# Four-layer model on one core: product-key expert products in one-pass parts, streamed tables, joined stage fronts

## The chip, the core and the metric

The kernel runs on one core of one Trainium2 chip. TensorE (PE) multiplies matrices, VectorE (DVE), ScalarE (ACT) and GpSimd (POOL) work on elements, SyncE's queue (SP) issues the transfers between DRAM and the on-chip memory (SBUF). Each engine runs its own program; semaphores order them. The metric is the device time of one execution in microseconds (us), less is better.

## The reference, cut to what matters

`x` is 64 sequences of 64 tokens with 256 channels (4096 tokens, float32). Four layers follow; each adds an attention and a feed-forward part to `x`, each on a layer norm of `x`:

```python
x = x + _L0_xattn_ref(_layernorm(x), ctx, mask, ...)   # attention with 8-bit rounded values
x = x + _L0_ffn_ref(_layernorm(x), Wq, keys, e_down, e_up)   # product-key experts
x = x + _L1_xattn_ref(...); x = x + _L1_ffn_ref(...)   # linear attention; 4-bit weights + LoRA
x = x + _L2_xattn_ref(...); x = x + _L2_ffn_ref(...)   # memory attention; self-attention + 16 experts
x = x + _L3_xattn_ref(...); x = x + _L3_ffn_ref(...)   # attention; 16 experts, two of them per token
```

The product-key part, which the change touches most:

```python
q1, q2 = (q[..., 0, :], q[..., 1, :])              # 4 heads, 64 wide each
s1, i1 = jax.lax.top_k(q1 . keys[:, :, 0], 8);  s2, i2 = jax.lax.top_k(q2 . keys[:, :, 1], 8)
all_scores = s1[..., :, None] + s2[..., None, :]   # 64 candidates
final_scores, pk_idx = jax.lax.top_k(all_scores, 8)
hidden = silu(x . e_down[final_indices]) * relu(final_scores)
out = hidden . e_up[final_indices]                 # 2048 experts, tables 2048 x 256
```

The dense part of layer 1 uses `w = (q - 7.5) * scale` for its two weights, plus a LoRA product of rank 16 for each, with 1024 hidden channels.

## The kernel before

The program is a row of stages, each a block of its own; between blocks all engines meet and the stage's semaphores are cleared. In order of time: first attention (0 to 370 us, 16 units of 256 tokens, `head_attention_stage` with `quant=True`), product-key experts (370 to 1201, `peer_stage`), linear attention, dense feed-forward (from 1424, `ffn_stage` named ffn4), memory attention, self-attention (from 1786), the 16 experts of layer 2 computed for every token in two passes (moe2a, moe2b), the last attention and the routed experts (4242 to 4604). `x` stays in SBUF throughout.

**Product-key stage** (L1030 to L1451). 4096 tokens in 16 tiles of 256. It gathers no rows: for every token it computes the sums of scores for all 2048 experts (16 first keys times 128 second ones), sets those under the eighth best to zero ("mask"), transposes that table on PE and multiplies it into the dense hidden values of all 2048 experts. A tile has 8 slots of 256 experts, and each engine's order is written out by hand (`tile_pe`, `tile_act`, `tile_dve`, `tile_gp`, L1331 to L1406); three tiles are in work at once. Per slot p:

- PE: the up product (`up_pe`, L1286: 8 float32 instructions of 256 columns), 16 transposes of a part of the table (`table_pe`, L1263), in some slots norm transposes, queries or scores, and the down product of slot p-2 (`down_pe`, L1313: 8 float32 instructions of 256 columns).
- ACT: SiLU (L1295), copy of the table part (L1271), in slots 0, 1, 4, 5 the sums of heads 0 and 2 (`sums_act`, L1191, 16 small activations each), score copies (L1175).
- DVE: activations times table (`weigh_dve`, L1304) of slot p-1, in slot 0 and 3 the search for the best (`pick_dve`, with the comparison L1219), in slots 1, 2, 5, 6 two masks each (`mask_dve`, L1246), in slot 2 the copy of the normalized input (`hand_over_dve`) and the norm of the tile after next (`norm_dve`), in slot 4 the residual.
- POOL: the sums of heads 1 and 3 (`sums_pool`, L1198) in slots 0, 1, 4, 5, and a power for the norm in slot 2 (`norm_pool`, L1114).

The two expert tables `wg` (for e_down) and `wd` (for e_up) are loaded once, as float32, and stay in SBUF.

**Split products.** The dense and layer-2 stages already run a float32 product as three one-pass products: each operand is split into a rounded part hi (type fp32r) and the rest lo = value - hi, and hi\*hi, hi\*lo and lo\*hi are summed (L576, L589). For the hidden values ACT rounds (L647) and POOL subtracts (L656).

**First attention.** POOL clears the block-diagonal value buffers `vbd` before its units (L2806 to L2813), and DVE waits for that. SP loads one context tile per unit. ACT's list of a unit and POOL's mask and bias work have slack that differs from unit to unit.

**Dense stage.** `dequant_block` (L138 to L196) is a block of its own: ten loads, then on DVE scaling of both tables (L179, L180), 12 additions of LoRA products (L186), on ACT two roundings (L194, L195), on DVE two subtractions (L189). After it the stage's own block starts with the norm of the first tile.

**Self-attention.** The raw weights come through four buffers `raw`, filled by SP at the start of the block, rounded by ACT (L1613) and subtracted by DVE (L1620).

**Routed stage.** PE computes the router's logits tile by tile (8 tiles, L3540) into one PSUM bank; after the last one DVE runs a chain of 20 steps over all of them (`route_dve`, L3554 to L3581) with one exponential on ACT (L3585) near its start; the counts on PE (L3601) wait for the chain's last cast (L3577).

## Time and profile before

| | |
|---|---|
| median of 3 runs | 4598.83 us |
| the runs | 4588.35, 4598.83, 4601.52 us |
| the profiled execution | 4605.66 us |
| its span | 4603.9 us, mean granted clock of TensorE 0.936 |
| PE busy | 4047.8 us (88%) |
| PE's weight loads | 3353.4 us (73%) |
| DVE busy | 2595.6 us (56%) |
| ACT busy | 2070.3 us (45%) |
| POOL busy | 903.5 us (20%) |

The shares are means over stages with different limits, so a stage has to be read by itself. A row of a windows view gives, for a stretch of the span, its length, then for each engine the busy time and in brackets the number of instructions, then the granted clock of TensorE (1.00 is 2.4 GHz, 0.50 is 1.2 GHz), the busy share of the DMA engines and GB/s. A row of a timeline gives start and length in us, the engine, the line of the kernel, the operation, what it writes and reads, the shapes and how many instructions were joined to the row; in square brackets the idle time of that engine ahead of it and what ended it. Lengths of PE rows include the time in which an instruction overlaps the next.

### The profile page before, as it was taken

What the parts mean: (1) busy time and instruction counts of PE and PEld (TensorE: products, weight loads), DVE (VectorE), ACT (ScalarE), POOL (GpSimd) and SP (SyncE); (2) the same over time, 40 slices, a digit from 0 to 9 for tenths busy, and PEclk for the clock granted to TensorE, in tenths of its full rate; (3) what the DMA queues carried; (4) which work ended last, traced back from release to release, by engine and by line L of the source; (5) the groups of instructions that cost most, each with busy time, mean ns of one, the idle gap of its engine ahead of it and who ended that gap; (6) DMA issues with size and microseconds to landing.
All of it is one profiled execution on the core that took longest, in us unless ns stands there. A gap on an engine that the chain in (4) does not pass through costs nothing. (4 is left out here: it accounts for less than half of the span.)

```text
span 4603.9 us, 74464 instructions
## 1 busy us (share of the span) xinstructions
PE 4047.8 (88%) x25328; PEld 3353.4 (73%) x25328; DVE 2595.6 (56%) x5873; ACT 2070.3 (45%) x5341; POOL 903.5 (20%) x738
## 2 busy tenths in 40 slices
PE   6885999999896877999999997999979998887791
PEld 4554899999774765877877886788868886665671
DVE  6887989899474337444444443433333333776533
ACT  6884666666222433433433333433333333675140
POOL 1112333233000430000000000222222222001245
PEclk8997999999997997999999998999989998998595
DMA  2001000000001003000000001100010000001244
GB/s 67 14 15 44 1 0 0 0 0 1 28 21 42 0 30 115 6 6 6 6 6 6 6 5 34 34 10 9 5 54 10 9 10 24 12 12 42 84 135 127
DMA packets 100309, 119.50 MB, mean 26 GB/s; under 512 B 13792, under 2 KB 81216, under 8 KB 99776
## 3 DMA queue, kind: packets, MB, share of 16 engines
q1 hardware_dynamic: 93168, 97.25, 6.6%
q0 software_dynamic: 6864, 18.75, 1.5%
q8 instruction: 150, 2.46, 0.2%
q14 instruction: 127, 1.04, 0.1%
HBM read 93.03 MB, written 22.94 MB: 25 GB/s over the span
## 5 line engine op out<-in xcount | busy, mean ns | idle before, releaser
L1191 ACT ACTIVATE peer_tab<-peer_sims 128x128 f32<-128x128 f32 x1024 | 305.7, 393 | 0.0
L1198 POOL TENSOR_TENSOR peer_tab<-peer_sims 128x2048 f32<-128x2048 f32 x64 | 246.3, 3868 | 289.3 <-ACT peer_sims L1175 260.1
L1246 DVE SCALAR_TENSOR_TENSOR peer_tab<-peer_tab,peer_th 128x2048 f32<-128x2048 f32 x128 | 298.2, 2371 | 2.6 <-ACT peer_tab L1191 2.3
L1263 PE MATMUL bank<-ident,peer_tab 128*128 128x128 f32 x2048 | 247.9, 275 | 24.6 <-DVE peer_tab L1246 24.6
L1263 PEld LDWEIGHTS bank<-ident,peer_tab 128*128 128x128 f32 x2048 | 234.5, 142 | 37.9 <-DVE peer_tab L1246 25.4
L1673 DVE COPY mha_ks<-bank 128x512 f32<-128x512 f32 x128 | 88.4, 691 | 302.5 <-PE bank L1638 300.1
L1778 PE MATMUL bank<-mha_wo,mha_oT 128*128 128x256 f32 x1024 | 243.6, 381 | 0.0
L1313 PE MATMUL bank<-peer_wd,peer_hh 128*128 128x256 f32 x1024 | 242.0, 379 | 1.2 <-DVE peer_hh L1304 1.2
L1286 PE MATMUL bank<-peer_hT,peer_wg 128*128 128x256 f32 x1024 | 242.7, 380 | 0.0
L668 DVE TENSOR_TENSOR moe2a_b<-moe2a_a,bank 128x512 f32<-128x512 f32 x104 | 71.4, 687 | 270.9 <-PE bank L576 239.8
L1286 PEld LDWEIGHTS bank<-peer_hT,peer_wg 128*128 128x128 f32 x1024 | 195.2, 191 | 26.6
L656 POOL TENSOR_TENSOR moe2a_hh_lo<-moe2a_hh,moe2a_hh_hi 128x512 fp32r<-128x512 f32 x104 | 141.1, 1357 | 370.0 <-ACT moe2a_hh_hi L647 352.9
L668 DVE TENSOR_TENSOR moe2b_b<-moe2b_a,bank 128x512 f32<-128x512 f32 x96 | 65.9, 687 | 250.5 <-PE bank L576 219.4
L1313 PEld LDWEIGHTS bank<-peer_wd,peer_hh 128*128 128x128 f32 x1024 | 188.2, 190 | 24.1 <-DVE peer_hh L1304 1.9
L1778 PEld LDWEIGHTS bank<-mha_wo,mha_oT 128*128 128x128 f32 x1024 | 186.0, 192 | 20.2
L656 POOL TENSOR_TENSOR moe2b_hh_lo<-moe2b_hh,moe2b_hh_hi 128x512 fp32r<-128x512 f32 x96 | 130.8, 1363 | 344.5 <-ACT moe2b_hh_hi L647 333.6
L1666 ACT ACTIVATE mha_vs<-bank 128x512 f32<-128x512 f32 x128 | 76.4, 597 | 253.4 <-PE bank L1652 253.2
L1295 ACT ACTIVATE peer_a<-bank 128x512 f32<-128x512 f32 x128 | 76.2, 595 | 210.9 <-PE bank L1286 169.6
L647 ACT ACTIVATE moe2a_hh_hi<-moe2a_hh 128x512 fp32r<-128x512 f32 x104 | 65.7, 632 | 226.8 <-DVE moe2a_hh L673 209.3
L1824 POOL TENSOR_TENSOR mha_r<-mha_ms,neghalf 128x4 f32<-128x4 f32 x8 | 8.1, 1008 | 811.8 <-DVE mha_ms L1813 811.8
L1661 ACT ACTIVATE mha_qs<-bank 128x512 f32<-128x512 f32 x128 | 76.6, 599 | 196.0 <-PE bank L1638 196.0
L1304 DVE TENSOR_TENSOR peer_hh<-peer_a,peer_cwT 128x512 f32<-128x512 f32 x128 | 121.9, 953 | 75.7 <-PE bank L1313 75.7
(533 smaller groups left out, 11101.1 us busy)
## 6 DMA issues: line engine op xcount, KB each, us to landing
m_y_rows<-moe_y SPq DMA_DIRECT2D x79, 128.0 KB, 1.7
att_ctxT<-in_ctxT_dram SPq DMA_DIRECT2D x32, 256.0 KB, 2.7
lin_ctxT<-in_ctxT_dram SPq DMA_DIRECT2D x16, 256.0 KB, 2.8
mem_ctxT<-in_ctxT_dram SPq DMA_DIRECT2D x16, 256.0 KB, 2.8
mem_ctx<-in_ctx_dram SPq DMA_DIRECT2D x16, 256.0 KB, 3.1
t_scratch<-mha_hTf SPq DMA_DIRECT2D x8, 512.0 KB, 4.6
moe2a_hTf<-t_scratch SPq DMA_DIRECT2D x8, 512.0 KB, 3.7
moe2b_hTf<-t_scratch SPq DMA_DIRECT2D x8, 512.0 KB, 3.7
```

Of the source, the lines that this page charges most:

```text
L656: nc.gpsimd.tensor_tensor(out=hhs[1][:, j % 2, :], in0=hh[:, j % 2, :], in1=hhs[0][:, j % 2, :], op=ALU.subtract).then_inc(lo_ready, 1)
L668: nc.vector.tensor_tensor(out=b[:, j % 2, :], in0=a[:, j % 2, :], in1=U[j % 2][:], op=ALU.mult).then_inc(b_ready, 1)
L1191: i = nc.scalar.activation(tab[g][h][:, b * P:(b + 1) * P], sims[:, g, h, P:2 * P], ACT.Identity, bias=sims[:, g, h, b:b + 1])
L1198: nc.gpsimd.tensor_tensor(out=tab[g][h][:].rearrange("p (a b) -> p a b", b=P), in0=sims[:, g, h, P:2 * P].unsqueeze(1).broadcast_to([P, NB ...
L1246: nc.vector.scalar_tensor_tensor(out=tab[g][h][:], in0=tab[g][h][:], scalar=th[:, g, h:h + 1], in1=tab[g][h][:], op0=ALU.is_ge, op1=ALU.mu ...
L1263: i = nc.tensor.matmul(TB[n % 2][:, j * P:(j + 1) * P], tab[g][h][:, blk * P:(blk + 1) * P], core.ident[:], start=(j == 0 and h == 0), sto ...
L1286: i = nc.tensor.matmul(GB[p % 2][:, n * PU:(n + 1) * PU], wg[:, c, blk * P:(blk + 1) * P], hT[par][:, c, :], start=(c == 0), stop=(c == C ...
L1304: nc.vector.tensor_tensor(out=hh[:, p % 2, :], in0=a[:, p % 2, :], in1=cwT[:, par, 2 * p:2 * p + 2, :].rearrange("p b t -> p (b t)"), op=A ...
L1313: i = nc.tensor.matmul(YB[par][:, g * D:(g + 1) * D], hh[:, p % 2, n * PU + g * P:n * PU + (g + 1) * P], wd[:, 2 * p + n, :], start=(p == ...
L1661: nc.scalar.activation(qs[:, s % 2, :], Q[:], ACT.Copy).then_inc(qs_ready, 1)
L1673: nc.vector.tensor_copy(ks[:, s % 2, :], K[:]).then_inc(ks_ready, 1)
L1778: i = nc.tensor.matmul(Y[g // 2][:, (g % 2) * D:(g % 2 + 1) * D], oT[:, s % 2, g * P:(g + 1) * P], wo[:, s, :], start=(s == 0 and g % 2 == ...
```

## The change

1. **Product-key stage.** The up and down products become three one-pass products each (12 instructions in place of 8). ACT rounds the hidden values of each slot (`round_act`), POOL subtracts (`low_pool`), in each slot behind the table copy on ACT, and on POOL behind `norm_pool` and ahead of the sums of slots 4 and 5; `down_pe` waits for the low part. DVE adds one subtraction per tile for the input's low part. The split tables are not kept in SBUF: SP loads for each slot 512 KB of each from DRAM, into rings of four (up) and two (down) buffers.
2. **First attention.** Per unit SP loads two pieces of the tables, ACT rounds them, POOL subtracts, SP stores hi and lo in DRAM. DVE waits only for two small constants of POOL; the clearing of `vbd` moves behind POOL's first norm.
3. **Dense stage.** `dequant_block` is gone. Its loads are issued by SP at the end of the linear attention (`DequantInputs`), its work is laid between the parts of the first tile's front in the stage's own block; the first up product waits for the first table's low part, the first down product for the second's.
4. **Self-attention.** The first four weight loads, the norm vectors and the causal mask are issued at the end of the memory attention (`AttentionInputs`); two waits take the place of one.
5. **Routed stage.** The routing chain runs in two portions, for tiles 0 to 5 and 6 to 7, with logits in two PSUM banks and two exponentials.

```diff
-def dequant_block(core, st, wgs, wds, bup, bdn, NB):
...
+class DequantInputs(Stage):
...
+    def load_sp(self, sp):
+        for out, in_ in self.up:
+            sp.dma_start(out, in_).then_inc(self.up_in, 16)
+        for out, in_ in self.small:
+            sp.dma_start(out, in_).then_inc(self.small_in, 16)
+        for out, in_ in self.down:
+            sp.dma_start(out, in_).then_inc(self.down_in, 16)
...
+            if relu and is_first(t):
+                pe.wait_ge(down_lo_made, 1)
...
+                lora_pe(pe, lora_up, 0)
...
+                lora_pe(pe, lora_down, N_UP)
+                pe.wait_ge(up_lo_made, 1)
...
+                    round_act(act, wg, wgs, N_UP, up_hi_made)
+                    round_act(act, wd, wds, N_LORA, down_hi_made)
...
+                    scale_dve(dve, wg, inputs.gq, inputs.gs, inputs.up_in, inputs.n_up)
+                    front_dve(dve, 0, 0, NORM)
+                    add_lora_dve(dve, lora_up, 0, 1)
+                    scale_dve(dve, wd, inputs.dq, inputs.ds, inputs.down_in, inputs.n_down)
+                    front_dve(dve, 0, 0, LOW)
+                    low_part_dve(dve, wg, wgs, up_hi_made, up_lo_made)
+                    add_lora_dve(dve, lora_down, N_UP, 2)
+                    low_part_dve(dve, wd, wds, down_hi_made, down_lo_made)
...
-    wg, wd = sb("wg", [P, C, E]), sb("wd", [P, NB, D])
+    WGR, WDR = 4, 2
+    wg = [sb(f"wg{i}", [P, 2, 2, C, P], FP32R) for i in range(WGR)]
+    wd = [sb(f"wd{i}", [P, 2, 2, D], FP32R) for i in range(WDR)]
+    PARTS = ((0, 0), (0, 1), (1, 0))
...
-        nc.vector.tensor_copy(hT[par][:], hTf[:]).then_inc(hT_ready, 1)
+        nc.vector.tensor_copy(hT[par][0][:], hTf[:]).then_inc(hT_hi, 1)
+        dve.wait_ge(hT_hi, t + 1)
+        nc.vector.tensor_tensor(out=hT[par][1][:], in0=hTf[:], in1=hT[par][0][:], op=ALU.subtract).then_inc(hT_ready, 1)
...
-            pe.wait_ge(tables_in, 32)
+        pe.wait_ge(wg_in[p % WGR], (t * (SLOTS // WGR) + p // WGR + 1) * 16)
...
-            blk = 2 * p + n
-            for c in range(C):
-                i = nc.tensor.matmul(GB[p % 2][:, n * PU:(n + 1) * PU], wg[:, c, blk * P:(blk + 1) * P], hT[par][:, c, :],
-                                     start=(c == 0), stop=(c == C - 1))
+            for m, (pw, ph) in enumerate(PARTS):
+                for c in range(C):
+                    i = nc.tensor.matmul(GB[p % 2][:, n * PU:(n + 1) * PU], wg[p % WGR][:, n, pw, c, :], hT[par][ph][:, c, :],
+                                         start=(m == 0 and c == 0), stop=(m == len(PARTS) - 1 and c == C - 1))
...
-        pe.wait_ge(hh_ready, t * SLOTS + p + 1)
+        pe.wait_ge(lo_ready, t * SLOTS + p + 1)
+        pe.wait_ge(wd_in[p % WDR], (t * (SLOTS // WDR) + p // WDR + 1) * 16)
...
-                i = nc.tensor.matmul(YB[par][:, g * D:(g + 1) * D], hh[:, p % 2, n * PU + g * P:n * PU + (g + 1) * P], wd[:, 2 * p + n, :],
-                                     start=(p == 0 and n == 0 and g == 0), stop=(p == SLOTS - 1 and n == 1), skip_group_check=True)
+                for m, (pw, ph) in enumerate(PARTS):
+                    i = nc.tensor.matmul(YB[par][:, g * D:(g + 1) * D], hhs[ph][:, p % 2, n * PU + g * P:n * PU + (g + 1) * P],
+                                         wd[p % WDR][:, n, pw, :], start=(p == 0 and n == 0 and g == 0 and m == 0),
+                                         stop=(p == SLOTS - 1 and n == 1 and m == len(PARTS) - 1), skip_group_check=True)
...
+    def round_act(act, t, p):
+        k = t * SLOTS + p
+        act.wait_ge(hh_ready, k + 1)
+        nc.scalar.activation(hhs[0][:, p % 2, :], hh[:, p % 2, :], ACT.Copy).then_inc(hi_ready, 1)
+
+    def low_pool(pool, t, p):
+        k = t * SLOTS + p
+        pool.wait_ge(hi_ready, k + 1)
+        nc.gpsimd.tensor_tensor(out=hhs[1][:, p % 2, :], in0=hh[:, p % 2, :], in1=hhs[0][:, p % 2, :],
+                                op=ALU.subtract).then_inc(lo_ready, 1)
+
+    def load_up_sp(sp, t, p):
+        if some(t * SLOTS + p - WGR + 1):
+            sp.wait_ge(g_ready, t * SLOTS + p - WGR + 1)
+        sp.dma_start(wg[p % WGR][:].rearrange("p n k c h -> p (n k c h)").bitcast(FP32), tables[0][:, p * 4 * D:(p + 1) * 4 * D]).then_inc(wg_in[p % WGR], 16)
+
+    def load_down_sp(sp, t, p):
+        if some(t * SLOTS + p - WDR + 1):
+            sp.wait_ge(hh_used, t * SLOTS + p - WDR + 1)
+        sp.dma_start(wd[p % WDR][:].rearrange("p n k d -> p (n k d)").bitcast(FP32), tables[1][:, p * 4 * D:(p + 1) * 4 * D]).then_inc(wd_in[p % WDR], 16)
 
...
+            tw, pw = lagged(t, p, 1)
+            if exists(t) and exists(tw):
+                round_act(act, tw, pw)
...
+                low_pool(pool, tw, pw)
...
-            sp.dma_start(wg[:], args["e_downT"].rearrange("(c p) h -> p c h", p=P)).then_inc(tables_in, 16)
...
+            for p in range(WGR - 1):
+                load_up_sp(sp, 0, p)
...
+                for p in range(SLOTS):
+                    q = p + WGR - 1
+                    if q < SLOTS:
+                        load_up_sp(sp, t, q)
+                    elif not (isinstance(t, int) and t == PT - 1):
+                        load_up_sp(sp, t + 1, q - SLOTS)
+                    load_down_sp(sp, t, p)
...
+class AttentionInputs(Stage):
...
+    def load_table_sp(sp, t, par):
+        if some(t - 1):
+            sp.wait_ge(t_lo, t - 1)
+        down = args["e_downT"].rearrange("(c p) h -> p c h", p=P)[:, :, bass.ds(t * P, P)]
+        sp.dma_start(t_raw[par][:, 0:D].rearrange("p (c h) -> p c h", c=C), down).then_inc(t_in[par], 16)
+        sp.dma_start(t_raw[par][:, D:2 * D], args["e_up"][bass.ds(t * P, P), :]).then_inc(t_in[par], 16)
+
+    def store_table_sp(sp, t, par):
+        sp.wait_ge(t_lo, t + 1)
+        for n, rows in enumerate(tables):
+            sp.dma_start(rows[:, bass.ds(t * 2 * D, 2 * D)].rearrange("p (k h) -> p k h", k=2),
+                         t_out[par][:, :, n * D:(n + 1) * D].bitcast(FP32)).then_inc(t_stored[par], 16)
+
+    def round_table_act(act, t, par):
+        act.wait_ge(t_in[par], (t // 2 + 1) * 32)
+        if some(t // 2):
+            act.wait_ge(t_stored[par], (t // 2) * 32)
+        nc.scalar.activation(t_out[par][:, 0, :], t_raw[par][:], ACT.Copy).then_inc(t_hi, 1)
+
+    def low_table_pool(pool, t, par):
+        pool.wait_ge(t_hi, t + 1)
+        nc.gpsimd.tensor_tensor(out=t_out[par][:, 1, :], in0=t_raw[par][:], in1=t_out[par][:, 0, :], op=ALU.subtract).then_inc(t_lo, 1)
 
...
+            round_table_act(act, t, par)
...
+        if is_int(t, -2):
+            blank_values_pool(pool)
...
+            low_table_pool(pool, t, par)
...
-            load_ctx(sp, 2, 0)
-            load_ctx(sp, 3, 1)
+            if tables is not None:
+                load_table_sp(sp, 0, 0)
+                load_table_sp(sp, 1, 1)
+            for t in (2, 3):
+                load_ctx(sp, t, t % 2)
+                if tables is not None:
+                    store_table_sp(sp, t - 2, t % 2)
+                    load_table_sp(sp, t, t % 2)
...
-            dve.wait_ge(zeroed, 3)
+            dve.wait_ge(fixed_set, 1)
...
+    PORTIONS = ((0, NT - 2), (NT - 2, NT))
+    route, shares = Chain(sem("route"), 17 * len(PORTIONS)), Chain(sem("shares"), 3)
...
+    def route_dve(dve, n):
+
+        t0, t1 = PORTIONS[n]
+        groups = slice(t0 * GT, t1 * GT)
+        NP = (t1 - t0) * GT
...
-            exp_act(act)
+                if t == NT - 1:
+                    exp_act(act, 0)
+            exp_act(act, 1)
...
-            route_dve(dve)
+            route_dve(dve, 0)
+            route_dve(dve, 1)
...
-            head_attention_stage(core, "att8", quant=True)
+            tables = [nc.dram_tensor(f"peer_{n}", (P, 16 * 2 * D), FP32, kind="Internal").ap() for n in ("down", "up")]
...
+            peer_stage(core, tables)
+        if 3 in stages:
+            inputs = DequantInputs(core, "ffn4_in", 8)
...
+            linear_attention_stage(core, inputs if 3 in stages else None)
...
+            ffn_stage(core, "ffn4", "relu", "ln", blocks=8, inputs=inputs, inputs_loaded=2 in stages)
+            inputs.close()
+        if 5 in stages:
+            attention_inputs = AttentionInputs(core)
...
+            memory_attention_stage(core, attention_inputs if 5 in stages else None)
...
+            self_attention_stage(core, attention_inputs, 4 in stages)
```

## Rows read from the trace of the kernel before

**Rows 1.** Windows view: first attention, product-key stage, one steady tile of it (columns above).

```profile
0.00:370.00 370.00, 282.70 (x2260) 186.02 (x2260) 280.95 (x656) 285.99 (x996) 45.60 (x65) 0.89 0.10 30
370.00:1201.00 831.00, 792.94 (x4672) 716.82 (x4672) 707.31 (x1360) 498.91 (x1393) 258.44 (x81) 0.98 0.02 7
787.00:836.00 49.00, 49.00 (x294) 44.47 (x293) 44.02 (x86) 31.08 (x89) 15.92 (x5) 1.00 0.00 0
```

**Rows 2.** Timeline of PE in the product-key stage, within a tile.

```profile
816.91 1.89 PE L1286 MATMUL bank<-peer_hT,peer_wg 128*128 128x256 f32 x8
818.63 1.91 PE L1263 MATMUL bank<-ident,peer_tab 128*128 128x128 f32 x16
```

**Rows 3.** Timeline of PE in the first MoE pass: first and last of 13 rows.

```profile
2902.52 0.29 PE L589 MATMUL bank<-moe2a_wd_hi,moe2a_hh_hi 128*128 128x256 f32 x1
...
2903.96 0.63 PE L576 MATMUL bank<-moe2a_hT_hi,moe2a_wg_hi 128*128 128x512 f32 x2
```

**Rows 4.** Single lines: duration ns min/median/max, first and last start; product-key stage, dense stage.

```profile
L1304 DVE TENSOR_TENSOR peer_hh<-peer_a,peer_cwT x107: 679/682/3221, 504.4 to 1149.8; 128x512 f32<-128x512 f32 x107
...
L1219 DVE TENSOR_SCALAR peer_past<-peer_i x27: 180/3470/3477, 508.9 to 1142.7; 128x32 f32<-128x32 uint32 x27
...
L1246 DVE SCALAR_TENSOR_TENSOR peer_tab<-peer_tab,peer_th x105: 2340/2344/2349, 499.0 to 1135.4; 128x2048 f32<-128x2048 f32 x105
...
L1198 POOL TENSOR_TENSOR peer_tab<-peer_sims x54: 3609/3794/4062, 504.7 to 1142.3; 128x2048 f32<-128x2048 f32 x54
...
L656 POOL TENSOR_TENSOR ffn_hh_lo<-ffn_hh,ffn_hh_hi x64: 1263/1291/1421, 1477.0 to 1694.3; 128x512 fp32r<-128x512 f32 x64
```

**Rows 5.** Timeline of the product-key stage: at its start, and in one tile.

```profile
425.59 7.96 DVE L1246 SCALAR_TENSOR_TENSOR peer_tab<-peer_tab,peer_th 128x2048 f32<-128x2048 f32 x2
...
426.13 10.89 POOL L1198 TENSOR_TENSOR peer_tab<-peer_sims 128x2048 f32<-128x2048 f32 x2 [7.82 <-ACT peer_sims L1175]
...
824.11 3.13 DVE L1304 TENSOR_TENSOR peer_hh<-peer_a,peer_cwT 128x512 f32<-128x512 f32 x1 [3.33 <-PE bank L1313]
...
833.63 4.78 ACT L1191 ACTIVATE peer_tab<-peer_sims 128x128 f32<-128x128 f32 x16
...
839.46 4.61 DVE L1246 SCALAR_TENSOR_TENSOR peer_tab<-peer_tab,peer_th 128x2048 f32<-128x2048 f32 x2
...
845.75 0.70 POOL L1114 TENSOR_TENSOR peer_rstd<-peer_ve,neghalf 128x2 f32<-128x2 f32 x1 [15.04 <-DVE peer_ve L1102]
```

**Rows 6.** Page: a costliest group (busy us, mean ns, idle); a DMA issue (KB, us).

```profile
L647 ACT ACTIVATE moe2a_hh_hi<-moe2a_hh 128x512 fp32r<-128x512 f32 x104 | 65.7, 632 | 226.8 <-DVE moe2a_hh L673 209.3
...
moe2a_hTf<-t_scratch SPq DMA_DIRECT2D x8, 512.0 KB, 3.7
```

**Rows 7.** Timeline at the start of the first attention, POOL and DVE.

```profile
17.22 0.10 POOL L2807 MEMSET att_fixed<- 128x1 f32 x1
...
20.11 0.75 DVE L2166 BATCH_NORM_STATS2 att_stats<-x 128x6 f32<-128x256 f32 x2 [4.06 <-POOL att_vbd L2813]
```

**Rows 8.** Timeline of the dense stage's front: first load to first product.

```profile
1424.62 0.38 SPq L165 DMA_DIRECT2D ffn_dq_gq<-in_up_q_dram  x1
...
1440.29 2.29 DVE L179 SCALAR_TENSOR_TENSOR ffn_dq_wg<-ffn_dq_gq,ffn_dq_gs 128x2048 f32<-128x2048 int32 x1 [17.92 <-DMA ffn_bdn<-in_bdn_dram]
...
1454.81 1.91 ACT L194 ACTIVATE ffn_wg_hi<-ffn_dq_wg 128x2048 fp32r<-128x2048 f32 x1 [34.22 <-DVE ffn_dq_wd L186]
...
1472.65 1.22 PE L576 MATMUL bank<-ffn_hT_hi,ffn_wg_hi 128*128 128x512 f32 x2 [2.43 <-DVE ffn_hT_lo L695]
```

**Rows 9.** Timeline of ACT at the start of the self-attention.

```profile
1797.11 1.34 ACT L1613 ACTIVATE mha_wv_hi<-mha_raw 128x512 fp32r<-128x512 f32 x2 [4.34 <-DMA mha_raw<-in_a_wv_dram]
```

**Rows 10.** Timeline of the routed stage: logits of tile 5, of 6 and 7; last cast.

```profile
4277.06 3.43 PE L3540 MATMUL bank<-moe_gw,moe_hTf 128*128 128x16 f32 x16
...
4282.08 6.85 PE L3540 MATMUL bank<-moe_gw,moe_hTf 128*128 128x16 f32 x32
...
4301.72 0.43 DVE L3577 CAST moe_oh<-moe_eq 128x512 bf16<-128x512 f32 x1
```

307 lines of the change are left out of this document (175 added, 132 removed).

## The prediction

> **What bounds the kernel now.** I read the busy times by stage first, since the program is a row of stages with a barrier between them, and each has its own limit. The product-key stage is by far the largest block that the change touches: 831 of 4603.9 us [rows 1]. Cut into its 49.0 us tiles (256 tokens each; 13 of the 16 repeat exactly), PE is busy for 49.0 of 49.0 us at the full clock, DVE for 44.0, ACT 31.1, POOL 15.9 [rows 1]. The reader is to see two things: PE sets the pace and waits for nobody, and DVE is only 5 us behind it. The one long wait of DVE in a tile is 3.3 us for PE, at 824.11 [rows 5].
>
> How much of DVE's 44.0 us is work? Its product of activations and table weights (L1304) takes 0.68 us, but once in 8 times 3.2 us, and the little comparison L1219 takes 0.18 or 3.47 us [rows 4]: 2.5 + 3.3 = 5.8 us a tile are stalls. What they wait for is seen best at the stage's start: POOL's addition starts at 426.13 while a mask of DVE (L1246, 2.34 us alone) runs; the two POOL operations then need 10.89 us, where two take 7.2 alone (3609 ns each at best), and the two masks begun at 425.59 take 7.96 us together where two take 4.61, a rest of POOL's operation more; at 824.11 L1304 stands still until POOL has ended [rows 4, 5]. So such pairs don't share: whichever starts holds the other for its whole length. DVE's own work is 44.0 - 5.8 = 38.2 us.
>
> **Product-key stage, PE.** The up product of a slot is 8 instructions in 816.91 to 818.63 = 1.72 us [rows 2]; the down product has the same count and shape and is taken the same. After it each is 12 one-pass products of 256 columns; the MoE stage runs exactly that: 12 from 2902.52 to 2903.96 = 1.44 us [rows 3]. Saved: 0.28 us x 16 in a tile = 4.5 us; PE needs 44.5 us. The Trainium skill (page "FP8 and Floating Point Precision", section "TensorE Precision Notes") counts true FP32 as four passes; three passes for four would make 1.29 us of 1.72, save 6.9 us a tile and leave PE 42.1. The row has 1.44, since its pace is 0.12 us an instruction; either way PE is no longer what is late.
>
> **Product-key stage, what is added.** Per tile ACT gets 8 roundings of 0.63 us, by the same rounding in the MoE stage [rows 6], = 5.0 (31.1 + 5.0 = 36.1 of busy time); DVE one subtraction of 128x512, 0.6 us by L1304's row; POOL 8 subtractions (`low_pool`) of 1.26 to 1.29 us by L656, the same operation in the dense stage [rows 4], 10.2 us. They all read two SBUF operands, against a DVE whose masks, products and small table steps do too.
>
> Sum of what can't run at once: masks 8 x 2.27 = 18.2, L1304 8 x 0.6 = 4.8, the rest of DVE of that kind about 6.3 (an estimate: candidates, thresholds, normalized rows, the new subtraction), POOL 4 x 3.5 + 8 x 1.2 = 23.6: 52.9 us. That is the least a tile can take if the exclusion holds, 3.9 above 49.0. DVE's work plus every stall, 38.2 + 0.6 + 5.8 + 8 x 1.2, is 54.2.
>
> Order adds to it. I walked one tile, each engine's program order with these durations, until the second tile repeated the first. DVE closes the loop:
> - own work 38.8 us;
> - stalls: the four additions of POOL now cost 1.7 + 0.9 + 0.9 + 3.5 = 7.0 (the first pair no longer lies together, because the subtraction of slot 7 goes between), five of the eight subtractions meet a DVE operation, 5 x 1.2 = 6.0: 13.0;
> - idle: in slot 4 ACT's rounding waits for DVE's product 3, and ACT's 4.78 us of sums [rows 5] stand behind it in its queue; the next mask needs them: rounding 0.6 + copies 1.2 + 4.8 less DVE's 1.2 of work = about 5; the scores' copy stands behind the rounding of slot 6: 1.2; the power on POOL 0.8, as now: 7.
>
> 58.8 us; I take 58, +9.0 a tile, because each idle term can shrink if something arrives earlier. In slot 2 POOL's `norm_pool` waits for DVE's variance, which comes after two masks (from 839.46; POOL waits 15.04 us until 845.75) [rows 5], and the subtraction of slot 1 is queued behind it; PE's down product 1 then waits some 8 us. PE has 58 - 44.5 = 13.5 us of room, so that costs nothing more while it stays inside. 14 tiles at +9.0 = 126, the last two (no new rows, less POOL work) +4: **+130 us**, bounds +55 (52.9) and +175 (all eight subtractions stall and 2 us more idle).
>
> The tables are streamed, 1 MB a slot. A 512 KB load lands in 3.7 us [rows 6]; the down table's is issued when down product p-2 is done and needed a slot and a half later, over 8 us. It stays hidden, 0; if the cover went, what lands late is added per slot, up to 2 us x 8.
>
> **First attention.** DVE no longer waits for the memsets: it starts at 20.11, where POOL's first two end at 17.32, 2.8 us earlier [rows 7]: -2.8. Each of 16 units gets a rounding (0.63) at the end of ACT's list, a subtraction on POOL behind its bias addition, two loads and two stores on SP's queue, which wait for the subtraction; the next context load stands behind them but is needed most of a unit later. ACT's 0.63 lies between the values' copy and the probabilities' copy: 0 to 0.63 a unit, -0 because nothing is taken off; I take 0.2, +3. If it is fully on the path +10.
>
> **Dense stage (ffn4).** Now its block starts at 1424.6, waits until 1440.29 for ten loads (17.92 us idle), dequantizes, rounds both tables, closes, and normalizes; the first product is at 1472.65 [rows 8], 48.0 us after the start. Then: loads issued in the linear attention's tail (its last context load is out long before), scaling 2.3 and rounding 1.9 by [rows 8], and, as estimates from the same stretch, norm 4.9, four additions 2.6, second scaling 2.3, low part of the input 1.2, low part of the weights 2.3: 17.5, and half a us until ACT's rounding is seen, 18. The first down product must still wait for the second table (rounding, subtraction): about one microsecond of it shows. 48.0 - 18 - 1 = **-29**; bounds -17.9 (the load wait alone) and -32.
>
> **Self-attention.** The first four loads come earlier, yet ACT's front stands behind the third pair of weights, which is in at 1797.11, after a wait of 4.34 us [rows 9]; that load is issued only when DVE has freed a buffer, and DVE frees it after its norm, which waits for no load. 0; bounds -3 and +1. The joined norm vectors add nothing.
>
> **Routed stage.** The routing chain on DVE runs from the last logits, 4282.08 + 6.85 = 4288.93, to 4302.15 [rows 10]: 13.2 us, 15 of its steps over 512 elements. Split 6:2, the first portion can start at 4280.5, when tile 5's logits end (4277.06 + 3.43) [rows 10]: 15 x 0.13 less and 0.8 more for an exponential behind ACT's last copies, until 4292.4; the second, 6.2 us, ends at 4298.6. **-3.5**, bounds -5 and 0 (what hides it is PE's logits of tiles 6 and 7).
>
> **Sum.** 130 - 2.8 + 3 - 29 + 0 - 3.5 = +98 us. The profiled execution took 4605.7 us (span 4603.9 and 1.8 around it): 4704. It lies 6.8 above the median of 4598.8, so the forecast for the median is **4697 us**, +2.1%.
>
> **The rivals.**
> 1. *Only the exclusion counts* (0.25): the engines slip until POOL works under DVE's other operations and the idle terms vanish. Tile 52.9 to 55: +55 to +84, total 4621 to 4655. For it: the tile now has stalls of 5.8 only, because POOL's sums have found DVE's searches. Against: a subtraction is released right after L1304, where the masks begin.
> 2. *PE stays the bound; faster* (0.18): the short subtractions slip between DVE's operations. Tile 45.5: -3.5 x 15 = -52, total 4513. For: DVE has PE's room in slot 7. Against: 52.9 > 49.
> 3. *Worse* (0.07): PE's gap in slot 3 lowers its clock. In the tile of [rows 1] the granted clock is 1.00, the 2.4 GHz level; at 1.2 GHz a slot's 44.5 / 8 = 5.6 us of PE's work would be 5.6 longer. With two or three such slots in a tile PE's room of 13.5 is used up and some 2 us a tile are added: 4730. The Trainium skill (page "TensorE: Matmul & The Clock Gate", section "HAM oscillation — how this bites in real kernels") warns of just such gaps between bursts; by it this rival would be the likeliest, but the first attention, where PE is busy for only 282.7 of 370.0 us, keeps a granted clock of 0.89 [rows 1], so I give it little.
> 4. *The stage cancels out* (0.05): a tile of 51, total within 0.3% of now. That is about what a measurement of this kernel can tell from no change.
>
> **How the numbers follow.** The forecast has 0.45, the rivals 0.25, 0.18, 0.07 and 0.05. Predicted is the likeliest, 4697. From 4580 to 4745 lie the forecast but for its edges, rival 1, most of rival 3 and rival 4: some 0.8. Slower by over 0.3% are the forecast and rivals 1 and 3, 0.45 + 0.25 + 0.07 = 0.77; within 0.3% rival 4, 0.05; faster rival 2, 0.18. Both signs: the likeliest case alone has 4660 to 4740.
>
> **What would show it.** Right, if the product-key tile is 56 to 60 us, DVE busy over 50 in it, masks of 3.5 us and more appear (now none over 2.35 in the steady tiles [rows 4]), POOL's 1.3 us subtractions show times over 2 us, and PE waits for `peer_hh_lo`. Wrong, if masks stay at 2.34 us, or PE is still 100% busy. The dense stage's first product should come 18 to 20 us after its block starts; the routing chain should show two exponentials and end about 10 us after the last logits. What would make all of it wrong is an exclusion that doesn't hold for these shapes, or loads that land late, seen as PE waits for DMA.

## The result, and the profile after

| | before | after |
|---|---|---|
| median | 4598.67 us (4 runs, 4588.35 to 4601.52) | 4714.89 us (4 runs, 4708.9 to 4716.2) |
| ratio | | 1.0254, 95% interval 1.0236 to 1.0272 |
| profiled execution: span, mean clock | 4603.9 us, 0.936 | 4713.6 us, 0.929 |
| busy: PE, DVE, ACT, POOL | 4047.8, 2595.6, 2070.3, 903.5 us | 4034.6, 2707.6, 2140.9, 1169.5 us |

The change makes the kernel slower by 116 us; 98 were forecast. PE has less to do, and every other engine more. Read by stage, from one stage's last instruction to the next one's (single instructions of both traces):

| stage | before | after | difference |
|---|---|---|---|
| first attention (end) | 368.3 | 378.4 | +10.1 |
| product-key experts | 831.5 | 969.3 | +137.8 |
| linear attention | 222.1 | 221.0 | -1.1 |
| dense stage with its front | 278.0 | 250.1 | -27.9 |
| memory attention to last attention | 2539.0 | 2539.7 | +0.7 |
| routed stage, to its chain's last cast | 63.3 | 59.8 | -3.5 |

The table adds up to +116.1, as the medians do; the two profiled executions themselves differ by 109.7 us, since the rest of the routed stage was 6 us shorter in the later one, with the same work. The prediction had already put the profiled execution of before 6.8 us above its median, and in the later runs that stage differed by up to 5 us between executions of equal code.

Windows of the changed kernel: first attention, product-key stage, and one tile of it (columns as in [rows 1]).

```profile
0.00:379.00 379.00, 287.65 (x2260) 190.06 (x2260) 287.50 (x656) 296.37 (x1012) 64.24 (x81) 0.89 0.21 62
381.00:1348.00 967.00, 782.99 (x5696) 750.36 (x5696) 810.98 (x1376) 560.24 (x1521) 506.37 (x209) 0.91 0.42 140
983.60:1042.00 58.40, 49.40 (x358) 47.56 (x358) 51.02 (x87) 34.94 (x97) 31.87 (x13) 0.91 0.43 144
```

Against [rows 1]: the tile is 58.4 us long where it was 49.0, PE is busy for 49.4 of them where it was for all, and its granted clock, 1.00 before, is 0.91: gaps have come in. (A clock of 0.91 over a stretch is a mean of the two levels: 1.2 GHz for 18% of it, 2.4 GHz for the rest.) DVE is at 51.0 (before 44.0), POOL at 31.9 (15.9). The tile as a mean of 13, from the 14 norm powers of POOL, one per tile; its first and last start are 466.8 and 1225.4:

```profile
L1142 POOL TENSOR_TENSOR peer_rstd<-peer_ve,neghalf x14: 699/700/702, 466.8 to 1225.4; 128x2 f32<-128x2 f32 x14
```

That is 758.6 / 13 = 58.36 us. The single lines that answer to [rows 4]:

```profile
L1276 DVE SCALAR_TENSOR_TENSOR peer_tab<-peer_tab,peer_th x106: 2335/2348/3389, 518.0 to 1278.8; 128x2048 f32<-128x2048 f32 x106
```

```profile
L1228 POOL TENSOR_TENSOR peer_tab<-peer_sims x52: 3602/3612/5666, 536.5 to 1264.4; 128x2048 f32<-128x2048 f32 x52
```

```profile
L1357 POOL TENSOR_TENSOR peer_hh_lo<-peer_hh,peer_hh_hi x106: 1260/1456/2648, 525.7 to 1284.6; 128x512 fp32r<-128x512 f32 x106
```

A mask never took over 2.35 us in the steady tiles before; now up to 3.39. POOL's addition takes up to 5.67 us, 4.06 before. The new subtraction takes 1.26 us by itself and up to 2.65 us when it has to wait for a mask. Waits in the tile (engine, what it waited for, us in total, times, longest):

```profile
ACT peer_hh_hi L1352 <- DVE peer_hh L1333: 17.8, 5, 4.5
...
PE bank L1344 <- POOL peer_hh_lo L1357: 9.0, 3, 4.0
...
DVE peer_tab L1276 <- ACT peer_tab L1221: 3.8, 1, 3.8
DVE peer_s L1239 <- ACT peer_sims L1205: 1.7, 1, 1.7
```

PE waits for POOL's low part, 9.0 us in three places. But PE has the room (two_products below shows it); what matters is that DVE waits for ACT's sums (3.8 us) and is held up in its own operations. The timeline of slots 4 and 5 shows both:

```profile
1001.61 0.63 ACT L1352 ACTIVATE peer_hh_hi<-peer_hh 128x512 fp32r<-128x512 f32 x1 [2.45 <-DVE peer_hh L1333]
...
1002.32 1.30 POOL L1357 TENSOR_TENSOR peer_hh_lo<-peer_hh,peer_hh_hi 128x512 fp32r<-128x512 f32 x1 [5.25 <-ACT peer_hh_hi L1352]
...
1003.10 4.78 ACT L1221 ACTIVATE peer_tab<-peer_sims 128x128 f32<-128x128 f32 x16
...
1008.00 5.66 DVE L1276 SCALAR_TENSOR_TENSOR peer_tab<-peer_tab,peer_th 128x2048 f32<-128x2048 f32 x2 [3.83 <-ACT peer_tab L1221]
...
1008.95 2.55 POOL L1357 TENSOR_TENSOR peer_hh_lo<-peer_hh,peer_hh_hi 128x512 fp32r<-128x512 f32 x1 [1.32 <-ACT peer_hh_hi L1352]
...
1011.46 5.66 POOL L1228 TENSOR_TENSOR peer_tab<-peer_sims 128x2048 f32<-128x2048 f32 x1
...
1013.58 3.56 DVE L1280 TENSOR_TENSOR peer_tab<-peer_tab,peer_rest 128x1 f32<-128x1 f32 x1
```

ACT has waited 2.45 us for DVE's product before it rounds (1001.61), and its 4.78 us of sums start only at 1003.10. DVE's mask needs them and starts at 1008.00, after 3.83 us of nothing. The subtraction issued at 1008.95 stands behind that mask (2.55 us where it needs 1.3) and then holds the second mask: two masks in 5.66 us where two take 4.61 [rows 5]. POOL's addition at 1011.46 stands behind the second mask and then holds a one-column addition of DVE for 3.56 us; that one takes 0.15 us otherwise.

Dense stage, from the start of its block to the first product; it answers to [rows 8]:

```profile
1571.79 2.29 DVE L840 SCALAR_TENSOR_TENSOR ffn_wg<-ffn_in_gq,ffn_in_gs 128x2048 f32<-128x2048 int32 x1 [2.61 <-PEq L89]
...
1583.17 1.91 ACT L850 ACTIVATE ffn_wg_hi<-ffn_wg 128x2048 fp32r<-128x2048 f32 x1
...
1590.65 1.22 PE L551 MATMUL bank<-ffn_hT_hi,ffn_wg_hi 128*128 128x512 f32 x2
```

Between the block's first instruction and the first product lie 18.9 us. Routed stage, which answers to [rows 10]: logits of tiles 6 and 7, the two exponentials, the last cast.

```profile
4401.79 6.85 PE L3692 MATMUL bank<-moe_gw,moe_hTf 128*128 128x16 f32 x32
...
4402.53 0.51 ACT L3746 ACTIVATE moe_pr<-moe_sh 128x384 f32<-128x384 f32 x1
...
4412.70 0.31 ACT L3746 ACTIVATE moe_pr<-moe_sh 128x128 f32<-128x128 f32 x1 [9.65 <-DVE moe_sh L3713]
...
4418.03 0.23 DVE L3735 CAST moe_oh<-moe_eq 128x128 bf16<-128x128 f32 x1
```

From the last logits (4408.64) to the end of the cast (4418.26) it is 9.6 us; it was 13.2. First attention, which answers to [rows 7]: DVE starts 3.1 us earlier.

```profile
16.98 0.75 DVE L2288 BATCH_NORM_STATS2 att_stats<-x 128x6 f32<-128x256 f32 x2 [1.22 <-POOL att_fixed L2959]
```

### The profile page after: what moved, and what is told of

Its sections match the earlier page's. It is cut to its first block and busy times, and to the rows that moved or that the text cites. A ratio compares the mean times of both kernels' runs of the same rounds, so it can differ in the third digit from the quotient of the medians.

```text
span 4713.6 us, 77777 instructions
## 1 busy us (share of the span) xinstructions
PE 4034.6 (86%) x26352; PEld 3385.9 (72%) x26352; DVE 2707.6 (57%) x5909; ACT 2140.9 (45%) x5486; POOL 1169.5 (25%) x882
## 5 line engine op out<-in xcount | busy, mean ns | idle before, releaser
L1276 DVE SCALAR_TENSOR_TENSOR peer_tab<-peer_tab,peer_th 128x2048 f32<-128x2048 f32 x128 | 345.0, 2735 | 61.3 <-ACT peer_tab L1221 61.1
L1344 PE MATMUL bank<-peer_wd,peer_hh_hi 128*128 128x256 f32 x1024 | 241.8, 318 | 149.8 <-POOL peer_hh_lo L1357 149.7
L1344 PEld LDWEIGHTS bank<-peer_wd,peer_hh_hi 128*128 128x128 f32 x1024 | 185.6, 211 | 167.1 <-POOL peer_hh_lo L1357 117.0
L1357 POOL TENSOR_TENSOR peer_hh_lo<-peer_hh,peer_hh_hi 128x512 fp32r<-128x512 f32 x128 | 227.3, 1776 | 279.1 <-ACT peer_hh_hi L1352 279.1
L1228 POOL TENSOR_TENSOR peer_tab<-peer_sims 128x2048 f32<-128x2048 f32 x64 | 269.6, 4215 | 27.3 <-ACT peer_sims L1205 22.7
L1352 ACT ACTIVATE peer_hh_hi<-peer_hh 128x512 fp32r<-128x512 f32 x128 | 81.0, 633 | 277.7 <-DVE peer_hh L1333 277.7
L1315 PE MATMUL bank<-peer_hT_hi,peer_wg 128*128 128x256 f32 x1024 | 203.9, 305 | 0.0
L1315 PEld LDWEIGHTS bank<-peer_hT_hi,peer_wg 128*128 128x128 f32 x1024 | 169.2, 214 | 0.2
```

The source lines that it names most:

```text
L1228: nc.gpsimd.tensor_tensor(out=tab[g][h][:].rearrange("p (a b) -> p a b", b=P), in0=sims[:, g, h, P:2 * P].unsqueeze(1).broadcast_to([P, NB ...
L1276: nc.vector.scalar_tensor_tensor(out=tab[g][h][:], in0=tab[g][h][:], scalar=th[:, g, h:h + 1], in1=tab[g][h][:], op0=ALU.is_ge, op1=ALU.mu ...
L1315: i = nc.tensor.matmul(GB[p % 2][:, n * PU:(n + 1) * PU], wg[p % WGR][:, n, pw, c, :], hT[par][ph][:, c, :], start=(m == 0 and c == 0), st ...
L1344: i = nc.tensor.matmul(YB[par][:, g * D:(g + 1) * D], hhs[ph][:, p % 2, n * PU + g * P:n * PU + (g + 1) * P], wd[p % WDR][:, n, pw, :], st ...
L1357: nc.gpsimd.tensor_tensor(out=hhs[1][:, p % 2, :], in0=hh[:, p % 2, :], in1=hhs[0][:, p % 2, :], op=ALU.subtract).then_inc(lo_ready, 1)
```

## The experiments

All start from the changed kernel. "Tile" is the mean of 13 tiles of the product-key stage, taken as above. The level moved a little from one group of runs to the next (the groups ran on different chips; the median of before was 4605.9 us with fronts_only, one_operand, low_on_dve and round_after_sums, 4596.5 with two_products, small_loads, sums_first and pool_rounds, 4607.2 with no_low, norm_last and up_only, 4596.0 with no_round_no_low), so kernels of different groups are compared by their ratio to before.

For the tiles DVE's time is split in three, as a mean of the same 13 tiles: idle is the length of the tile less DVE's busy time; stalls are, for each of its instructions, the duration less what the same instruction takes where nothing holds it, in whichever of these traces that is seen; own work is what is left. The last clause matters for one instruction: the sum of candidates (`peer_cand`) takes 0.98 us both times in every tile of before, and 0.41 us in the changed kernel where POOL is not in the way. So before had 6.9 us of stalls, not 5.8, and 37.0 us of own work.

| kernel | tile | own | stalls | idle | ratio to before (95% interval) |
|---|---|---|---|---|---|
| before | 48.9 | 37.0 | 6.9 | 5.0 | 1 |
| changed kernel | 58.4 | 38.0 | 12.7 | 7.7 | 1.0254 (1.0236 to 1.0272) |
| one_operand | 55.1 | 38.0 | 9.8 | 7.3 | 1.016 (1.0139 to 1.018) |
| no_low | 54.1 | 38.0 | 7.6 | 8.5 | 1.0116 (1.0095 to 1.0137) |
| no_round_no_low | 48.4 | 37.8 | 7.2 | 3.3 | 0.9935 (0.9912 to 0.9957) |
| low_on_dve | 59.3 | 43.0 | 7.4 | 9.0 | 1.029 (1.0269 to 1.0311) |
| round_after_sums | 61.5 | 38.1 | 11.8 | 11.6 | 1.0337 (1.0315 to 1.0358) |
| sums_first | 61.4 | 37.9 | 16.7 | 6.8 | 1.0344 (1.0314 to 1.0374) |
| two_products | 58.3 | | | | 1.0241 (1.021 to 1.0271) |
| small_loads | 58.4 | | | | 1.0258 (1.0228 to 1.0288) |
| norm_last | 58.4 | | | | 1.0271 (1.0249 to 1.0292) |
| up_only | 49.0 | 37.8 | 6.9 | 4.3 | 0.9983 (0.9973 to 0.9993) |
| pool_rounds | 58.4 | | | | 1.026 (1.023 to 1.0289) |
| fronts_only | 48.9 | | | | 0.992 (0.9903 to 0.9936) |

**1. fronts_only: all of the change but the product-key stage and its tables, which are those of before.**

```diff
-            head_attention_stage(core, "att8", quant=True, tables=tables)
+            head_attention_stage(core, "att8", quant=True)
...
-            peer_stage(core, tables)
+            peer_stage(core)
```

(`peer_stage` itself is put back as it was before; the attention, called without tables, keeps DVE's earlier start)

> The changed kernel with the product-key stage, its tables and the first attention's table work as before; all else of the change stays. Theory (the product-key stage alone made the loss): first attention -2.8, dense stage -28, routed stage -3.6 against before, 4598.7 - 34.4 = 4564 us, 4555 to 4575. Rival (the joined fronts and the early loads cost something elsewhere that the stage totals hide): over 4585.

Measured: 4567.64 us (4 runs) against 4605.9, -38 us; expected -34. The loss is all in the product-key stage and its preparation, and this version is faster than both kernels. Its attention ended at 365.0 us (before 368.3), its product-key stage took 831.5 us as before.

**2. two_products: PE does a third less in the products.**

```diff
-    PARTS = ((0, 0), (0, 1), (1, 0))
+    PARTS = ((0, 0), (0, 1))
```

> The changed kernel without the third one-pass product (low part of the tables times high part of the values) in the up and the down product; output less exact. PE has 16 x 0.48 = 7.7 us a tile less to do. Theory (DVE closes the loop, PE has room): tile 58.4 within 0.5, total 4707 to 4722. Rival (PE with its lowered clock, 0.91, is part of the loop): tile 54 to 57, total under 4695.

```profile
984.93:1043.21 58.28, 43.01 (x292) 41.15 (x292) 49.70 (x86) 34.87 (x95) 31.68 (x13) 0.85 0.42 144
```

PE's busy time falls from 49.4 to 43.0 us and the tile stays (58.33 against 58.36); the total is 4708.40 us, as expected. PE's time falls by less than the 7.7 us expected, since its granted clock falls too, from 0.91 to 0.85: its longest gap in the tile grew from 4.0 to 5.3 us. With this much more room for PE changing nothing, PE is not part of what sets the tile, neither by its products nor by its lower clock.

**3. small_loads: an eighth of the bytes.**

```diff
+    def width(t):
+        return 4 * D if isinstance(t, int) and t == 0 else D // 2
...
-        sp.dma_start(wg[p % WGR][:].rearrange("p n k c h -> p (n k c h)").bitcast(FP32), tables[0][:, p * 4 * D:(p + 1) * 4 * D]).then_inc(wg_in[p % WGR], 16)
+        sp.dma_start(wg[p % WGR][:].rearrange("p n k c h -> p (n k c h)")[:, 0:width(t)].bitcast(FP32), tables[0][:, p * 4 * D:p * 4 * D + width(t)]).then_inc(wg_in[p % WGR], 16)
```

(and the same for the other table)

> The changed kernel, but after the first tile each load of a table carries an eighth of its bytes, so that old values stay in the buffers; output wrong by that. Theory (streaming is hidden): tile 58.4, total within 5 us of 4715. Rival (140 GB/s of transfers slow the engines' work or land late): tile 57 or less, total under 4695.

```profile
993.02:1051.33 58.31, 49.02 (x356) 47.17 (x356) 50.91 (x86) 34.86 (x95) 31.86 (x13) 0.91 0.06 18
```

The transfers fall from 144 to 18 GB/s, and tile (58.37 us), busy times and total (4716.41) stay. Streaming is hidden; the loads landed in 4.4 and 3.6 us (page of the changed kernel):

```profile
peer_wg<-peer_down SPq DMA_DIRECT2D x128, 512.0 KB, 4.4
peer_wd<-peer_up SPq DMA_DIRECT2D x128, 512.0 KB, 3.6
```

**4. one_operand: POOL copies where it subtracted.**

```diff
-        nc.gpsimd.tensor_tensor(out=hhs[1][:, p % 2, :], in0=hh[:, p % 2, :], in1=hhs[0][:, p % 2, :],
-                                op=ALU.subtract).then_inc(lo_ready, 1)
+        pool.sem_inc(passed, 1)
+        nc.gpsimd.tensor_copy(hhs[1][:, p % 2, :], hh[:, p % 2, :]).then_inc(lo_ready, 1)
```

> The changed kernel, but POOL's low part in the product-key stage is a copy with one operand (hh_lo <- hh) where it was a subtraction with two; same count, place and size. The output is off by the product that this gets wrong. Theory (POOL and DVE operations with two SBUF operands exclude each other): the five stalls that the subtractions cause in a tile, 5.1 of its 58.4 us in the changed kernel's trace, vanish: tile 53.3 (52 to 55), total 4715 - 15 x 5.1 = 4638. Rival (the order of the queues and POOL's own time count, whatever the operands): tile 58.4, total 4715.

The tile fell to 55.1 us, by 3.3 of the expected 5.1, and the total to 4678.23 where 4638 was expected: neither theory nor rival. The cause is in its timeline:

```profile
977.75 4.97 DVE L1276 SCALAR_TENSOR_TENSOR peer_tab<-peer_tab,peer_th 128x2048 f32<-128x2048 f32 x2 [4.95 <-ACT peer_tab L1221]
...
978.80 1.78 POOL L1358 CAST peer_hh_lo<-peer_hh 128x512 fp32r<-128x512 f32 x1 [1.95 <-ACT peer_hh_hi L1352]
...
993.12 0.62 POOL L1358 CAST peer_hh_lo<-peer_hh 128x512 fp32r<-128x512 f32 x1 [3.58 <-ACT peer_hh_hi L1352]
```

A copy that meets no mask takes 0.6 us (993.12). The one issued at 978.80, inside a mask, takes 1.78, and the two masks around it take 4.97 us together where two take 4.61. So a one-operand copy on POOL waits for the mask and holds the next one, exactly as the subtraction does, only for its own shorter time. The theory named the wrong condition: the exclusion doesn't ask for two operands on POOL's side. That the stalls scale with the length of POOL's operation (about 1.0 us each against 0.35) is what the table shows: 12.7 us fall to 9.8. They would fall further, but in five of the 13 tiles an addition of POOL now holds one of DVE's products for some 3 us more, in place of as much idle time.

**5. no_low: POOL's subtraction left out.**

```diff
-        nc.gpsimd.tensor_tensor(out=hhs[1][:, p % 2, :], in0=hh[:, p % 2, :], in1=hhs[0][:, p % 2, :],
-                                op=ALU.subtract).then_inc(lo_ready, 1)
+        pool.sem_inc(lo_ready, 1)
```

> The changed kernel with POOL's subtraction in the product-key stage left out: POOL only passes the semaphore on after ACT's rounding, and the low part of the hidden values stays zero (output less exact). PE's 12 instructions, ACT's rounding and the streaming stay. Theory (the subtractions' stalls, 6.1 us of the tile's 13.0, go and nothing takes their place): tile 58.4 - 6.1 = 52.3, 50.5 to 53; total 4715 - 15 x 6.1 = 4624. Rival (the rounding and the longer way to the down product are as bad by themselves, and idle time fills up what the stalls leave): tile 55 or more, total over 4665.

Between the two: 54.1 us, 4659.67. The stalls fell by 5.1 us, where 6.1 was expected, and idle time came up by 0.8. The subtraction costs 4.3 us a tile, and something else costs 5.2.

**6. no_round_no_low: ACT's rounding left out as well.**

```diff
-        pe.wait_ge(lo_ready, t * SLOTS + p + 1)
+        pe.wait_ge(hh_ready, t * SLOTS + p + 1)
...
-            if exists(t) and exists(tw):
-                round_act(act, tw, pw)
...
-            if exists(t) and exists(tw):
-                low_pool(pool, tw, pw)
```

> As the run without POOL's subtraction, and ACT's rounding in the product-key stage is left out too; the down product waits for DVE's product as before the change and multiplies zeros (output wrong by that). PE's 12 instructions, the streaming and the input's split stay. That run had a tile of 54.1 with 7.3 us of stalls and 7.5 of idle time on DVE. Theory (DVE's idle time, 5 us of it ahead of a mask, is ACT's sums standing behind the rounding): it falls to the 2.6 of the run with the up product alone: tile 54.1 - 5 = 49 or less, 47 to 49.5; total 4660 - 15 x 5.5 = 4577, 4555 to 4590. Rival (the idle time comes from PE's longer product or the streaming): tile 52 or more, total over 4625.

Windows of one tile, first of the run before and then of this one:

```profile
1006.20:1060.37 54.17, 46.45 (x356) 45.17 (x356) 45.39 (x86) 34.62 (x95) 16.36 (x5) 0.94 0.45 155
```

```profile
948.37:996.50 48.13, 44.82 (x359) 43.24 (x358) 45.17 (x86) 30.95 (x87) 15.91 (x5) 1.00 0.50 175
```

The tile falls to 48.4 us, the total to 4566.94, as the theory had it. Idle time goes from 8.5 to 3.3 us, PE's clock from 0.94 to 1.00. ACT is busy for 3.7 us less; the tile is 5.7 shorter. So the step of rounding is the larger part of the loss, and not by its own time: with it DVE waits for ACT and ACT for DVE in turn. The edit takes three things away together, and their shares of the 5.7 us were not separated: the rounding's place in ACT's queue ahead of the sums; POOL's wait for it ahead of its own additions (in the tile of no_low shown here POOL waits up to 9.1 us for the rounding with an addition next in its list); and one engine on the way from DVE's product to the down product. Even with all of it gone the tile gains only 0.5 us on before, though PE's 44.8 us of work would allow 4: DVE, with 37.8 us of work and 7.2 of stalls, is now as late as PE, and the two wait for each other.

**7. low_on_dve: the subtraction on DVE.**

```diff
-        nc.gpsimd.tensor_tensor(out=hhs[1][:, p % 2, :], in0=hh[:, p % 2, :], in1=hhs[0][:, p % 2, :],
+        nc.vector.tensor_tensor(out=hhs[1][:, p % 2, :], in0=hh[:, p % 2, :], in1=hhs[0][:, p % 2, :],
```

(called in DVE's list at the end of each slot, and no more in POOL's)

> The changed kernel with the product-key stage's eight subtractions a tile on DVE (behind its other work of the slot) where POOL did them. Theory (exclusion): DVE's own work 38.6 + 8 x 0.68 = 44.1, stalls by POOL's four additions 5.8 to 6.9, idle 5 to 7: tile 55 to 58, at or a little under 58.4, total 4665 to 4710. Rival (no exclusion; DVE was late by its own work): 58.4 + 5.4 = 63.8 a tile, total 4795.

59.3 us, 4738.31 us: 1.3 us a tile and 28 us in total over the theory's range, and far from the rival's 63.8 and 4795. DVE's own work rose by 5.0 us, its stalls fell by 5.3, and idle time rose by 1.3, which the theory did not have. So the subtraction on POOL costs DVE about as much as if DVE did it.

**8. round_after_sums: the sums of slots 4 and 5 ahead of the rounding on ACT.**

```diff
-            if exists(t) and exists(tw):
+            if exists(t) and exists(tw) and p not in (4, 5):
                 round_act(act, tw, pw)
...
                 sums_act(act, t + 1, 1, 2 * (p - 4))
+            if exists(t) and exists(tw) and p in (4, 5):
+                round_act(act, tw, pw)
```

> The changed kernel with ACT's rounding in slots 4 and 5 moved behind its sums. Theory (DVE's idle 3.8 us ahead of its mask in slot 5 is ACT's sums standing behind a rounding that waits for DVE): tile 58.4 - 3.8 = 54.6 or a little over it, total 4715 - 15 x 3.5 = 4662. Rival (the subtraction that comes later then meets another DVE operation, or the down product is late): tile within 1 us of 58.4.

Neither: 61.5 us, 4759.77, slower by 3.1 a tile. In its timeline:

```profile
967.56 4.79 ACT L1221 ACTIVATE peer_tab<-peer_sims 128x128 f32<-128x128 f32 x16
...
972.24 0.62 ACT L1352 ACTIVATE peer_hh_hi<-peer_hh 128x512 fp32r<-128x512 f32 x1
972.38 2.35 DVE L1276 SCALAR_TENSOR_TENSOR peer_tab<-peer_tab,peer_th 128x2048 f32<-128x2048 f32 x1 [3.16 <-ACT peer_tab L1221]
...
972.94 2.92 POOL L1357 TENSOR_TENSOR peer_hh_lo<-peer_hh,peer_hh_hi 128x512 fp32r<-128x512 f32 x1 [9.73 <-ACT peer_hh_hi L1352]
...
975.82 3.61 POOL L1228 TENSOR_TENSOR peer_tab<-peer_sims 128x2048 f32<-128x2048 f32 x1
...
979.46 3.35 DVE L1276 SCALAR_TENSOR_TENSOR peer_tab<-peer_tab,peer_th 128x2048 f32<-128x2048 f32 x1 [4.73 <-POOL peer_tab L1228]
```

ACT's sums start at 967.56, but the rounding is now at 972.24; POOL's subtraction, 9.73 us idle ahead of it, is issued at 972.94, just into a mask, and POOL's additions stand behind it in its queue. DVE waits 3.16 us for ACT's sums as before and then 4.73 us for POOL's.

**9. sums_first: the same turn on POOL too.**

```diff
+            if p in (4, 5) and exists(t + 1):
+                sums_pool(pool, t + 1, 1, 2 * (p - 4) + 1)
             if exists(t) and exists(tw):
                 low_pool(pool, tw, pw)
-            if p in (4, 5) and exists(t + 1):
-                sums_pool(pool, t + 1, 1, 2 * (p - 4) + 1)
```

> The changed kernel with the sums of slots 4 and 5 ahead of the rounding on ACT and, unlike in the run before, also ahead of the subtraction on POOL. Theory (in that run POOL's subtraction, waiting 9.7 us for the late rounding, held up POOL's sums, and DVE's second mask waited 4.7 us for these): with both orders turned DVE's idle of 3.2 and 4.7 us goes and the additions stall DVE for 5.8 to 6.9 as ever: tile 54 to 56, total 4650 to 4680. Rival (the down product, two slots behind, then waits so long that DVE waits for a hidden-value buffer): tile 58 or more.

61.4 us, 4755.86: the rival. The idle time ahead of the masks did go (1.2 us are left of 7.9), but the down product comes so late that DVE waits for the buffer of hidden values, which the product has to free:

```profile
989.38 0.68 DVE L1333 TENSOR_TENSOR peer_hh<-peer_a,peer_cwT 128x512 f32<-128x512 f32 x1
993.74 3.55 DVE L1333 TENSOR_TENSOR peer_hh<-peer_a,peer_cwT 128x512 f32<-128x512 f32 x1 [3.68 <-PE bank L1344]
```

3.68 us idle, and then 3.55 us for a product of 0.68, since POOL's addition has started meanwhile. The stalls are 16.7 us, the most of all. Turning the order round doesn't remove the loss; it comes back at another place, and larger.

**10. norm_last: the subtraction of slot 1 ahead of the norm power on POOL.**

```diff
-            if p == 2 and exists(t + 2):
-                norm_pool(pool, t + 2)
...
             if exists(t) and exists(tw):
                 low_pool(pool, tw, pw)
+            if p == 2 and exists(t + 2):
+                norm_pool(pool, t + 2)
```

> The changed kernel with POOL's subtraction of slot 1 ahead of its norm power in slot 2 where it stood behind it. Theory (PE's wait of 4.0 us behind it lies inside PE's room): tile 58.4 within 0.5, total 4707 to 4722. Rival (that wait is part of the loop): tile 57.4 or less, total under 4700.

The tile is 58.44 us, as expected, though PE's longest wait for a low part fell from 4.0 to 2.9 us: that wait was free. The total, 4731.0, is over the range given, but before stood at 4607.2 in that group: the ratio, 1.0271, is within the interval of the changed kernel's.

**11. pool_rounds: three edits in three stages.**

```diff
-        nc.scalar.activation(t_out[par][:, 0, :], t_raw[par][:], ACT.Copy).then_inc(t_hi, 1)
+        nc.gpsimd.tensor_copy(t_out[par][:, 0, :], t_raw[par][:]).then_inc(t_hi, 1)
...
-            linear_attention_stage(core, inputs if 3 in stages else None)
-            ffn_stage(core, "ffn4", "relu", "ln", blocks=8, inputs=inputs, inputs_loaded=2 in stages)
+            linear_attention_stage(core)
+            ffn_stage(core, "ffn4", "relu", "ln", blocks=8, inputs=inputs)
```

The rounding of the tables stands in POOL's list; the routed stage is that of before.

> Three edits to the changed kernel in three stages, read by stage. First attention: POOL rounds the tables as well as subtracting; ACT has none of it. Theory (ACT's rounding is on the path): stage 375.8 to about 366 us. Rival (POOL's subtraction or the four transfers): 375 or more. Dense stage: its loads are issued in its own block again, the joined front stays. Theory: of the 28 us gained, the load wait gives 15 to 18 back, 10 to 13 stay. Routed stage as before the change: +3 to +4. Total 4715 - 10 + 17 + 3 = 4725.

The total was 4717.11 us, 4725 expected. First attention: it ended at 369.5 us, 378.4 in the changed kernel; about 366 was expected. One execution is little, since with this attention unchanged the other kernels ended it at 375.4 to 379.1 us, and two_products even at 371.1. But those differences go with the granted clock of the stage: 0.89 in the three executions that ended at 379.0 and 379.1, 0.90 in the six from 375.4 to 378.4, 0.92 in two_products. pool_rounds had 0.90, and at that clock it is 6 to 9 us earlier than the six. So 6 to 9 of the some 13 us that the table work costs here are the rounding's place in ACT's queue; that rests on one execution of pool_rounds. Routed stage: 347.7 us; with the split chain it took 343.9 to 349.0 in twelve profiles, before it 351.8 in one: nothing can be told from its total, only from the chain. Dense stage:

```profile
1563.45 0.38 SPq L160 DMA_DIRECT2D ffn_in_gq<-in_up_q_dram  x1
...
1571.50 2.29 DVE L840 SCALAR_TENSOR_TENSOR ffn_wg<-ffn_in_gq,ffn_in_gs 128x2048 f32<-128x2048 int32 x1 [10.31 <-DMA ffn_in_gs<-in_up_s_dram]
...
1592.49 1.22 PE L551 MATMUL bank<-ffn_hT_hi,ffn_wg_hi 128*128 128x512 f32 x2
```

The first product comes 29.0 us after the block's first load (before 48.0; in the changed kernel 18.9 after the block starts). The loads' early issue gives 10 us, where 15 to 18 were expected. Here the prediction's picture was off: of the gain, 19 us are the joined front and only 10 the early loads, since the joined front waits for two of the ten loads (10.31 us idle on DVE) and not for all of them (17.92 [rows 8]). The stage as a whole says the same: 260.0 us, 250.1 in the changed kernel.

**12. up_only: the up product alone in three one-pass products.** The down product stays float32 with its table in SBUF, and nothing per slot is rounded or subtracted; one table of two is split and streamed.

```diff
-    wd = [sb(f"wd{i}", [P, 2, 2, D], FP32R) for i in range(WDR)]
+    wd = sb("wd", [P, NB, D])
...
-        pe.wait_ge(lo_ready, t * SLOTS + p + 1)
+        pe.wait_ge(hh_ready, t * SLOTS + p + 1)
```

> Only the up product in three one-pass products; the down product is float32 as before, its table in SBUF, with no rounding and no subtraction per slot. The first attention prepares one table, half the data; joined fronts as in the change. Theory: PE sets the pace again, 49.0 - 8 x 0.28 = 46.8 us a tile; DVE has 38.2 + 0.7 + stalls 5.8 = 44.7. Stage -15 x 2.2 = -33 against fronts_only, first attention +3 to +8: 4567.6 - 33 + 5 = 4540, 4532 to 4555. Rival (DVE's stalls and its idle time close the loop at 48 to 49): 4562 or more.

```profile
945.00:993.73 48.73, 46.86 (x326) 44.03 (x325) 44.85 (x86) 30.94 (x87) 15.91 (x5) 1.00 0.28 87
```

4595.41 us (10 runs), -0.17% against before and 0.6% slower than fronts_only; the theory (4540) is refuted by the total, and the rival, a tile of 48 to 49, holds. PE's busy time is the 46.8 us expected and DVE's mean the 44.7, but this tile is 48.7 long: DVE waits for a buffer that PE frees, loses 2.5 us in that product to POOL's addition, and PE then waits for the product. Three of 13 tiles take 50.3 us, so the mean is 49.0 and the gain nothing. The first attention, with half of the table work, ended at 366.4 us, 1.4 after that of fronts_only, where +3 to +8 was expected. Most of the 28 us that it loses to fronts_only lie in a stage that was not touched (last section).

## Why the prediction was right

The change cost 116 us where 98 were forecast. Of the 18 us between, 10 lie in the first attention and 8 in the product-key stage.

**The tile (term +9.0 a tile, stage +130).** Measured +9.4 and +137.8. DVE closed the loop as in the walk: own work 38.8 forecast, 38.0 measured; stalls 13.0 and 12.7; idle 7 and 7.7. In the tile shown the additions' 7.0 us were 6.9, but the forecast 1.7 + 0.9 + 0.9 + 3.5 were 0.67 and 2.84 in the search and 3.42 at the one-column addition; the subtractions' 5 x 1.2 = 6.0 were six of about 1.0. The idle time ahead of the mask in slot 5 was 3.8 where 5 stood, the one before the search 1.7 where 1.2 stood. So the kinds of loss were right, and that their sums met within 0.7 us is partly luck. The starting point was read a little wrong as well: before has 6.9 us of stalls, not 5.8, as said above the table. PE's wait in slot 3, forecast as some 8 us, was 4.0. And the upper bound, +175, leaves out the 2 us of idle time that it names: 14 x (9.0 + 3.6) is 176, and with those 2 us 204.

**Its reason.** The walk had two causes in it, and the text leaned on the exclusion. Leaving out the subtraction took 4.3 us off the tile (no_low), leaving out ACT's rounding, with the waits of POOL and PE for it, 5.7 more (no_round_no_low). So the rounding step, whose price stood in the walk under "idle", is the larger part. Rival 1, only the exclusion counts and the idle terms vanish, forecast 52.9 to 55; it was wrong for the same reason: the idle terms didn't vanish.

**How the exclusion works** was half right: masks and POOL's operations don't share; in the rows shown the one that comes second takes longer by the rest of the first. That POOL's operation must have two operands was a guess, and one_operand refuted it for a copy.

**PE.** That 12 one-pass products take 1.44 us where 8 float32 took 1.72 held: without gaps the tile's PE work was 44.8 us (no_round_no_low), 44.5 forecast. In the changed kernel PE was busy for 49.4 because its clock was 0.91 (1.00 in [rows 1]): PE waits 4.0 us until 994.03, and from 995.3 to 998.6 the granted clock is 0.50, the 1.2 GHz level; from 1000 to 1037, without a gap over 1.4 us, it is 1.00. The Trainium skill (page "TensorE: Matmul & The Clock Gate", section "HAM oscillation — how this bites in real kernels") warned of this, and the granted clock agrees. So rival 3 had the clock right and its effect wrong: PE did not become the bound, since giving it 6.4 us more room left the tile the same (two_products). The Trainium skill's rule about float32 as four passes (page "FP8 and Floating Point Precision", section "TensorE Precision Notes") would have put PE's work at 42.1, an estimate; the measured 44.8 decides for the row's 0.12 us an instruction.

**Streaming at 0**: right (small_loads).

**First attention (-2.8 + 3, up to +10).** The start was right (3.1 us earlier), the sum was mis-sized: the stage became 10.1 us longer, so the table work costs 13 us, 0.8 a unit, where 0.2 a unit stood. Even the bound, 0.63 a unit, was under it. ACT's rounding was priced as if it had slack. With the rounding on POOL the stage ended 6 to 9 us earlier than at the same granted clock with it on ACT (pool_rounds, one execution), so about half of the cost or more is its place in ACT's queue; which wait passes it on is open, and so is the rest.

**Dense stage (-29)**: -27.9. The first product comes 19 us after the block's start, 18 were forecast. The lower bound, -17.9 for the load wait alone, rested on a wrong split: the early loads bring 10 and the joined work 19 (pool_rounds).

**Self-attention (0)**: 0. **Routed stage (-3.5)**: the chain ends 9.6 us after the last logits, 13.2 before, -3.6.

**Signs announced.** Tile 56 to 60, DVE over 50, subtractions over 2 us, PE waiting for `peer_hh_lo`, two exponentials: all seen. Masks of 3.5 us: not quite, 3.39 at most.

## What to carry to other kernels

When the bound engine is made faster, look at what the operands for it cost on engines that are 10% behind it: here 4.5 us of PE a tile were bought with 16 small operations on ACT and POOL, and the tile grew by 9.4. An operation of 0.63 us put into another engine's queue is priced by what stands behind it there and waits for whom, not by its length; walking one tile of all queues until it repeats gave the growth of the tile within 5%. In this kernel the parts outside the product-key stage are worth keeping (joined fronts, early loads, split chain): 0.8% faster than before (fronts_only, ratio 0.9903 to 0.9936), and by the two ratios 3.3% faster than the changed kernel. The 3.6 us of the split chain are seen in the chain alone.

## What was not expected of the hardware

**A stage that was not touched became 21 us longer or more.** In up_only the self-attention took 1089.8 us, 1065.0 to 1068.5 in all other kernels, before among them. PE's waits in that stage, with no releaser that the profile shows, at one line of the stage, the same in both kernels: up_only, then fronts_only.

```profile
PE bank L1707 <- issue: 20.0, 5, 4.3
```

```profile
PE bank L1680 <- issue: 4.9, 5, 1.2
```

Five waits, up to 4.3 us each where they take 1.2. They explain 15 of the 23.7 us by which the stage is longer than in fronts_only (1066.1). All five stand at one spot: between the last product of one pass of PE's loop over the tiles and the first of the next (2028.4, 2162.2, 2297.7, 2431.4 and 2567.1), once for each return to the loop's start. The code of that stage is the same; what differs is the code that lies ahead of it. Why PE waits longer there is open. Changes of a few tenths of a per cent in this kernel have to be checked in the untouched stages too.

**A copy on POOL with one operand takes part in the exclusion** with DVE's masks (1.78 us where 0.62 are usual), and on DVE's side even a one-column addition is held (3.56 us for 0.15), and so is a `TENSOR_SCALAR` of four columns with one input (`peer_th`, 3.02 us for 0.17). The searches are not: in the changed kernel the eight `MAX8` from 1026.15 take 1.65 us beside an addition of POOL that runs from 1026.18 to 1029.79, and no `MAX8` or `FIND_INDEX8` of the steady tiles takes over 0.30 us. That is the work of DVE under which POOL can be laid.

**With less work PE was granted a lower clock** (0.91 to 0.85, two_products), so that 7.7 us less of products gave only 6.4 us less of busy time.
